# Attention: each unit's row maximum is rescaled on ScalarE instead of on VectorE

## The chip, the cores and the metric

One Trainium2 chip, and one of its cores does the whole computation. A core has five engines that run their own instruction streams and meet only at semaphores: TensorE (PE, matmuls and transposes; its weight loads are shown as PEld), VectorE (DVE), ScalarE (ACT), GpSimd (POOL) and SyncE (SP, which issues most of the DMAs). The metric is the device time of one execution in microseconds (us); the figure for a kernel is the median of its runs.

## The reference

The input `x` is 16 x 256 rows of 128 numbers. Three blocks are added to it in turn: a feed-forward block of eight experts (each row goes to the one expert with the highest gate logit), an attention block over 512 context keys with 8 heads, and the same feed-forward block again. All three read the layer norm of the current rows. The attention, which is what the change touches, is

```python
sim = einsum('hid,hjd->hij', qh, kh) * SCALE
mean = mean(sim, axis=-1)
sim = (sim - mean) * 1.5 + mean
attn = softmax(sim, axis=-1)
out = einsum('hij,hjd->hid', attn, vh)
```

for 4096 queries, 8 heads and 512 keys: 4096 x 8 x 512 scores, of which each row of 512 goes through a softmax.

## The kernel before

The span has three stages. In the first 143 us the attention weights are prepared and the first feed-forward block runs, 39 tiles of 128 rows one after another, sorted by expert. From 143 to about 634 us the attention runs. The rest is the second feed-forward block, whose routing (which row goes to which expert, at which place) is worked out while the attention runs.

The attention is cut into 256 *units*. Unit u belongs to group g = u // 32 (a group is 4 tiles of 128 queries, 512 queries together), to head h = (u // 4) % 8 and to tile or key chunk i = u % 4. For softmax the unit is one tile of 128 queries against all 512 keys of one head. For the product with the values the unit is one chunk of 128 keys against all 512 queries of the group, so it can start only when the four softmax units of its head are done.

Precision is that of fp32, made from fp16 pairs: a high part and a low part are kept of each operand and three matmuls are added (`three`, lines 1561 to 1563). So that the fp16 parts use their whole range, the operands are multiplied by powers of two that are computed from bounds on the data; `MUN` is the reciprocal power of two for the scores, one number for each partition in SBUF, that undoes this.

Each engine has a function `slot(n)` that is called for n = 0, 1, 2, ... and does a part of several units. What stands first in the function is issued first, and an engine never passes an instruction that waits:

- PE: scores of unit n (3 matmuls, lines 1561 to 1563, into one of three PSUM banks; waits until the exponential of unit n-3 is done). Then the value product of unit n-8 (3 matmuls, the same lines; at the first unit of a head it waits for `probsT_lo` of that head's last unit, n-5). Then the four transposes of unit n-3's probabilities (line 1785; they wait for the normalised probabilities of that unit, and for `probsT_lo` of unit n-5).
- DVE: `neg_max`, minus the row maximum of unit n's scores (line 1443), then `neg_max_unscaled`, that times `MUN` (line 1446), then `probsT_lo` of unit n-4 (line 1452, the transposed probabilities minus their fp16 high part; waits for ACT's high part), then `row_inv` of unit n-1 (line 1457).
- ACT: `probs` of unit n = exp(MUN * scores + neg_max_unscaled) with the row sum as a by-product (line 868), then `probsT_hi` of unit n-3 (line 877, the fp16 high part of the transposed probabilities).
- POOL: `probs` of unit n-1 times `row_inv` (line 642).

At fixed places of each group of 32 slots further work hangs on the end of a slot. On DVE: layer-norm statistics of the next group (slots 7 to 11 and 13), the residual rows of the last group (15 to 18), `xT_lo` (21, 22), statistics of the new rows (23 to 27), and the routing of the finished group (29 to 31 and 3 to 5 of the next). On ACT: `o_evac` (slot 8, line 896), four `ln_norm` (14 to 17, line 782), `ln_keep` (20, line 793), `x2T_evac` (22, line 902). On PE: four transposes each in slots 14, 19 and 20, the gate logits in 24 (line 1828) and the ranks in slot 1. On POOL: a power of 4 numbers a row in slots 12 and 28 (line 626 is the latter), for which DVE waits in slots 13 and 29.

The change touches the attention part of ACT's and DVE's `slot`. The semaphore `neg_max` is raised by line 1443 and `neg_max_ready` by line 1446; both `NM` and `NMS` have four columns, used in turn.

Of the kernel before, what the change touches and what calls it, by code (L numbers as in the profile page):

```python
# [8 lines left out]
def macaron_kernel(nc, x, context, Wq, Wk, Wv, Wout, bout, gate_w, gate_b, expert_bias, w1, b1, w2, b2, out):  # L9
# [13 lines left out]
    ALU = mybir.AluOpType  # L23
    ACT = mybir.ActivationFunctionType
# [39 lines left out]
    with ctx:  # L64
        def sb(name, shape, dt, where=ctx):
            return where.enter_context(nc.sbuf_tensor(name, shape, dt))

        def sem(name):
            return ctx.enter_context(nc.semaphore(name))
# [48 lines left out]
        NM = sb("neg_max", [P, 4], fp32)  # L118
        NMS = sb("neg_max_unscaled", [P, 4], fp32)
# [51 lines left out]
        with ExitStack() as att:  # L171
# [18 lines left out]
        MUN, VUN = (UNI[:, k:k + 1].bitcast(fp32) for k in range(2))  # L190
# [30 lines left out]
        neg_max_ready = sem("neg_max_unscaled_ready")  # L221
# [41 lines left out]
        scores, neg_max, probs, row_inv, normed = (sem("scores"), sem("neg_max_ready"), sem("probs_ready"),  # L263
                                                   sem("row_inv_ready"), sem("probs_normed"))
# [52 lines left out]
        def score_bank(u):  # L317

            return BK[u % 2] if u < FIRST_UNITS else BK[(6, 0, 1)[(u - FIRST_UNITS) % 3]]

        def turn_bank(job):

            return 4 + job % 2 if job else 1

        def unit(u):
            return 0 <= u < UNITS

        def after(n, s, back):

            g = n // HG - back  # L330
            return [g] if n % HG == s and 0 <= g < NG else []

        def ahead(n, s):

            return after(n, s, -1)
# [8 lines left out]
        def wait_rows(eng, r, j):  # L344

            if j >= CLOSE:
                eng.wait_ge(s_close, (SLOTS - CLOSE) * r + j - CLOSE + 1)
            else:
                eng.wait_ge(s_fin, CLOSE * r + j + 1)
# [337 lines left out]
        def _(act):  # L687
# [89 lines left out]
            def ln_norm(job, tiles_):  # L777
                act.wait_ge(ln_shift, job + 1)
                if job:
                    act.wait_ge(ln_T, job)  # L780
                for i in tiles_:
                    last = act.activation(XN[:, i, :], ROWS[:, G * job + i, 0:D], ACT.Identity, bias=SH[:, i:i + 1],
                                          scale=RS[:, i:i + 1])
                if i == G - 1:
                    last.then_inc(ln_xn, 1)
# [5 lines left out]
            def ln_keep(job, bank):  # L791
                act.wait_ge(ln_T, job + 1)
                act.activation(AXH[:, job % 2, :], BK[bank][:, :], ACT.Copy, scale=2.0 ** X_BITS)\
                    .then_inc(xT_hi, 1)
# [66 lines left out]
            def slot(n):  # L861
                if unit(n):
                    if n == 0:
                        act.wait_ge(s_hb, SLOTS)
                    act.wait_ge(neg_max_ready, n + 1)
                    if n >= 4:
                        act.wait_ge(pT_ps, n - 3)
                    act.activation(PR[:, n % 4, :], score_bank(n)[:, :], ACT.Exp, bias=NMS[:, n % 4:n % 4 + 1],  # L868
                                   scale=MUN, accum_out=SU[:, n % 4:n % 4 + 1]).then_inc(probs, 1)
                if unit(n - LAG_T):  # L870
                    u = n - LAG_T
                    act.wait_ge(pT_ps, u + 1)
                    if u == 0:
                        wait_rows(act, 0, SLOTS - 1)
                    if u % G == 0 and u // G >= 2:
                        act.wait_ge(av, G * (u // G) - G)
                    act.activation(PTH[:, (u // G) % 2, :, (u % G) * P:(u % G + 1) * P],  # L877
                                   BK[2 + u % 2][:, :].rearrange("p (c q) -> p c q", c=KC), ACT.Copy)\
                        .then_inc(pT_hi, 1)
                for i in range(G):  # L880
                    for g in ahead(n, 14 + i):
                        ln_norm(g, [i])
                for g in ahead(n, 20):
                    ln_keep(g, turn_bank(g))
                for g in after(n, 8, 1):
                    o_evac(g)
                for g in after(n, 22, 1):
                    x2T_evac(g)

            def o_evac(g):  # L890
                if g == 0:
                    act.wait_ge(bout_in, 16)
                act.wait_ge(av, HG * (g + 1))
                if g:
                    act.wait_ge(x2_logits, g)
                act.activation(XNT[:, :], BK[4 + g % 2][:, :], ACT.Identity, bias=BO[:, 0:1], scale=VUN)\
                    .then_inc(o_kept, 1)

            def x2T_evac(g):
                act.wait_ge(x2_T, g + 1)  # L900
                act.wait_ge(oT_ps, g + 1)
                act.activation(XNT[:, :], BK[router_bank(g, STAT_STEP)][:, :], ACT.Copy).then_inc(x2T_kept, 1)
# [7 lines left out]
        def _(dve):  # L910
            v = nc.vector
# [306 lines left out]
            def ln_stats(job, tiles_):  # L1218
                for i in tiles_:
                    last = v.bn_stats(BN[0][:, i, :], ROWS[:, G * job + i, 0:D])  # L1220
                if i == G - 1:
                    last.then_inc(ln_bn, 1)
# [12 lines left out]
            def ln_shift_of(job):  # L1235

                dve.wait_ge(ln_rstd, job + 1)
                v.scalar_tensor_tensor(out=SH[:, :], in0=MV[:, :, 0], scalar=-1.0, in1=RS[:, :],
                                       op0=ALU.mult, op1=ALU.mult).then_inc(ln_shift, 1)
# [200 lines left out]
            def slot(n):  # L1440
                if unit(n):
                    dve.wait_ge(scores, n + 1)
                    v.tensor_reduce(NM[:, n % 4:n % 4 + 1], score_bank(n)[:, :], AX.X, ALU.max, negate=True)\  # L1443
                        .then_inc(neg_max, 1)
                    dve.wait_ge(neg_max, n + 1)
                    v.tensor_scalar(NMS[:, n % 4:n % 4 + 1], NM[:, n % 4:n % 4 + 1], MUN, None, ALU.mult)\  # L1446
                        .then_inc(neg_max_ready, 1)
                if unit(n - LAG_T - 1):
                    u = n - LAG_T - 1
                    dve.wait_ge(pT_hi, u + 1)  # L1450
                    at = (slice(None), (u // G) % 2, slice(None), slice((u % G) * P, (u % G + 1) * P))
                    v.tensor_tensor(PTL[at], BK[2 + u % 2][:, :].rearrange("p (c q) -> p c q", c=KC),  # L1452
                                    PTH[at], ALU.subtract).then_inc(pT_lo, 1)
                if unit(n - 1):
                    u = n - 1
                    dve.wait_ge(probs, u + 1)
                    v.reciprocal(RI[:, u % 4:u % 4 + 1], SU[:, u % 4:u % 4 + 1]).then_inc(row_inv, 1)  # L1457

                for i in range(G):
                    for g in ahead(n, 7 + i):  # L1460
                        if n == 7:
                            dve.wait_ge(x1_in[1], 16 * (NG - 2))
                        if g == NG - 1 and i == 0:
                            dve.wait_ge(x1_in[2], 16)
                        ln_stats(g, [i])
                for g in ahead(n, 11):
                    ln_moments(g)
                for g in ahead(n, 13):
                    ln_shift_of(g)
                for half in range(2):  # L1470
                    for g in ahead(n, 21 + half):
                        xT_low(g, turn_bank(g), slice(half * 2 * P, (half + 1) * 2 * P))

                for i in range(G):
                    for g in after(n, 15 + i, 1):
                        new_row(g, i)
                    for g in after(n, 23 + i, 1):
                        x2_stats(g, i)
                for g in after(n, 27, 1):
                    x2_moments(g)  # L1480
                for g in after(n, 30, 1):
                    x2_shift_of(g)
                for i in range(3):
                    for g in after(n, 29 + i, 1):
                        onehot(g, range(3 * i, min(3 * i + 3, 8)))
                    for g in after(n, 3 + i, 2):
                        positions(g, [i])
                for i in range(14):
                    for g in after(n, 6 + i, 2):
                        if g == EARLY_GROUP:  # L1490
                            early_table(i)
# [395 lines left out]
```

## Time and profile before

| | us |
|---|---|
| median of 3 runs | 739.3 |
| the three runs | 738.98, 739.3, 742.73 |
| the profiled execution, its own time | 743.87 |
| its span in the trace | 742.0 |
| granted TensorE clock over the span, mean | 0.985 of full |

The trace is of one execution on the core. Its times count from the start of the span. Busy time of an engine is not its need: where a row says that an engine sat idle before an instruction, the number in brackets is that idle time and the name behind the arrow is what it waited for. An instruction may start before the end of the one ahead of it on the same engine, because they are pipelined; two starts tell the pace, and one duration tells the latency.

### The profile page before, as it was taken

The page shows a single profiled execution, that of the slowest core. Times are in us where ns is not written, and L with a number is a line of the kernel's source. Part 1 is how long each engine was busy: PE and PEld are TensorE (multiplying, and loading weights), DVE is VectorE, ACT ScalarE, POOL GpSimd, SP SyncE. Part 2 cuts the span into 40 slices and gives each one's busy share as a digit, 9 for nine tenths or more (in the row PEclk, how much of TensorE's full clock was granted, in tenths as well). Part 3 has the DMA queues.
Part 4 walks back from the last instruction along what each step waited for, and adds up shares of the span by engine and source line. Part 5 has one row for each costly group of instructions (what it writes and reads, how often), then busy time and mean ns, then how long its engine had stood idle before and what let it go on. Part 6 is the DMA issues. An engine that isn't in the chain of part 4 may idle for free.

```text
span 742.0 us, 15538 instructions
## 1 busy us (share of the span) xinstructions
PE 695.0 (94%) x4376; PEld 472.7 (64%) x4376; DVE 655.7 (88%) x1910; ACT 523.4 (71%) x1219; POOL 374.1 (50%) x507
## 2 busy tenths in 40 slices
PE   9988999989999999999999999999999998889992
PEld 7767888746556555655655655655565564669991
DVE  6989999998898999899899989899989987788882
ACT  4786777578778678778767867867876775546661
POOL 5066998344344345346346435534633633486662
PEclk9989999999999999999999999999999999999996
DMA  9951332210000000000000000000000011232210
GB/s 246 348 149 32 80 86 74 63 41 0 1 1 1 1 5 12 2 0 15 1 1 12 5 1 7 10 0 5 12 1 1 16 45 57 101 90 62 58 47 5
DMA packets 31794, 31.50 MB, mean 42 GB/s; under 512 B 5049, under 2 KB 26183, under 8 KB 31200
## 3 DMA queue, kind: packets, MB, share of 16 engines
q1 hardware_dynamic: 27360, 23.91, 11.0%
q0 software_dynamic: 3520, 6.40, 3.2%
q8 instruction: 38, 0.62, 0.4%
q14 instruction: 44, 0.36, 0.2%
q10 hardware_dynamic: 832, 0.21, 0.1%
HBM read 20.96 MB, written 10.47 MB: 42 GB/s over the span
## 4 chain that ended last, share of the span: by engine, by line
PE 47%; DVE 39%; issue 5%; POOL 2%; DMA 2%; ACT 1%; DVEq 1%; POOLq 0%; another core or an unknown queue 0%; SPq 0%; ACTq 0%
PE bank L1561 10%; DVE neg_max L1443 10%; PE bank L1563 9%; PE bank L1562 9%; DVE probsT_lo L1452 9%; PE bank L1785 9%; PE bank L1610 3%; DVE neg_max_unscaled L1446 3%; DVE hT_lo L1297 3%; PE bank L1596 2%; DVE slot_rows L1280 2%; DVE h L1276 2%; PE bank L1613 1%; DVE slot_rows L1289 1%; DMA rows<-in_L_attn_x 1%
## 5 line engine op out<-in xcount | busy, mean ns | idle before, releaser
L642 POOL TENSOR_SCALAR probs<-probs,row_inv 128x512 f32<-128x512 f32 x256 | 178.2, 697 | 266.1 <-DVE row_inv L1457 254.9
L868 ACT ACTIVATE probs<-bank,neg_max_unscaled,unscale_bits 128x512 f32<-128x512 f32 x256 | 199.2, 778 | 115.3 <-DVE neg_max_unscaled L1446 112.8
L1443 DVE TENSOR_REDUCE neg_max<-bank 128x1 f32<-128x512 f32 x256 | 175.9, 687 | 23.9 <-PE bank L1563 18.4
L1452 DVE TENSOR_TENSOR probsT_lo<-bank,probsT_hi 128x512 f16<-128x512 f32 x256 | 174.4, 681 | 3.3 <-ACT probsT_hi L877 3.2
L1785 PEld LDWEIGHTS bank<-ident,probs 128*128 128x128 f32 x1024 | 126.0, 141 | 65.9 <-issue 18.1
L1785 PE MATMUL bank<-ident,probs 128*128 128x128 f32 x1024 | 155.1, 274 | 8.6 <-DVE probsT_lo L1452 7.0
L877 ACT ACTIVATE probsT_hi<-bank 128x512 f16<-128x512 f32 x256 | 150.3, 587 | 3.2 <-PE bank L1785 3.2
L1561 PE MATMUL bank<-probsT_hi,vw_hi 128*128 128x512 f16 x256 | 98.1, 383 | 7.6 <-DVE probsT_lo L1452 6.7
L1562 PE MATMUL bank<-probsT_lo,vw_hi 128*128 128x512 f16 x256 | 97.5, 381 | 0.0
L1563 PE MATMUL bank<-probsT_hi,vw_lo 128*128 128x512 f16 x256 | 97.4, 380 | 0.0
L1561 PE MATMUL bank<-m_hi,xT_hi 128*128 128x512 f16 x256 | 97.0, 379 | 0.0
L1563 PE MATMUL bank<-m_hi,xT_lo 128*128 128x512 f16 x256 | 97.0, 379 | 0.0
L1562 PE MATMUL bank<-m_lo,xT_hi 128*128 128x512 f16 x256 | 97.0, 379 | 0.0
L1610 PE MATMUL bank<-w_hi_lo,hT_hi 128*128 x312 | 83.9, 346 | 10.5 <-DVE hT_lo L1297 6.3
L1613 PE MATMUL bank<-w_hi_lo,hT_lo 128*128 x312 | 69.7, 224 | 0.0
L1610 PEld LDWEIGHTS bank<-w_hi_lo,hT_hi 128*128 128x128 f32 x312 | 59.3, 190 | 16.1 <-issue 16.0
L818 ACT ACTIVATE hT_hi<-bank 128x512 fp32r<-128x512 f32 x78 | 46.6, 598 | 26.5 <-PE bank L1596 17.3
L1446 DVE TENSOR_SCALAR neg_max_unscaled<-neg_max,unscale_bits 128x1 f32<-128x1 f32 x256 | 54.8, 214 | 9.0
L1276 DVE TENSOR_TENSOR h<-bank,b 128x512 f32<-128x512 f32 x78 | 53.6, 687 | 9.6 <-PE bank L1563 7.4
L1613 PEld LDWEIGHTS bank<-w_hi_lo,hT_lo 128*128 128x128 f32 x312 | 60.3, 193 | 0.0
L1561 PEld LDWEIGHTS bank<-probsT_hi,vw_hi 128*128 128x128 f16 x256 | 25.0, 98 | 54.0 <-DVE probsT_lo L1452 30.9
L1297 DVE SCALAR_TENSOR_TENSOR hT_lo<-bank,hT_hi 128x512 fp32r<-128x512 f32 x78 | 53.0, 680 | 4.1 <-issue 2.1
(239 smaller groups left out, 1189.9 us busy)
## 6 DMA issues: line engine op xcount, KB each, us to landing
b<-in_L_ffn_b SPq DMA_DIRECT2D x4, 1024.0 KB, 9.1
x_packed<-slot_rows SPq DMA_DIRECT2D x39, 65.5 KB
slot_rows<-slots SPq DMA_DIRECT2D x39, 65.5 KB
x_stats<-rows SPq DMA_DIRECT2D x4, 524.0 KB, 10.5
rows<-x_packed SPq DMA_DIRECT2D x8, 262.0 KB, 2.6
rows<-in_L_attn_x SPq DMA_DIRECT2D x4, 512.0 KB, 8.6
w_lo<-in_L_ffn_w SPq DMA_DIRECT2D x8, 256.0 KB, 6.6
w_hi_lo<-in_L_ffn_w SPq DMA_DIRECT2D x8, 256.0 KB, 8.6
```

The costliest lines, as they stand in the source:

```text
L642: pool.tensor_scalar(PR[:, u % 4, :], PR[:, u % 4, :], RI[:, u % 4:u % 4 + 1], 2.0 ** P_BITS, ALU.mult, ALU.mult).then_inc(normed, 1)
L868: act.activation(PR[:, n % 4, :], score_bank(n)[:, :], ACT.Exp, bias=NMS[:, n % 4:n % 4 + 1], scale=MUN, accum_out=SU[:, n % 4:n % 4 + 1]) ...
L877: act.activation(PTH[:, (u // G) % 2, :, (u % G) * P:(u % G + 1) * P], BK[2 + u % 2][:, :].rearrange("p (c q) -> p c q", c=KC), ACT.Copy)\
L1443: v.tensor_reduce(NM[:, n % 4:n % 4 + 1], score_bank(n)[:, :], AX.X, ALU.max, negate=True)\
L1446: v.tensor_scalar(NMS[:, n % 4:n % 4 + 1], NM[:, n % 4:n % 4 + 1], MUN, None, ALU.mult)\
L1452: v.tensor_tensor(PTL[at], BK[2 + u % 2][:, :].rearrange("p (c q) -> p c q", c=KC), PTH[at], ALU.subtract).then_inc(pT_lo, 1)
L1561: pe.matmul(out_, wh, mh, start=start, stop=False)
L1562: pe.matmul(out_, wh, ml, start=False, stop=False)
L1563: return pe.matmul(out_, wl, mh, start=False, stop=stop)
L1610: pe.matmul(BK[6 + j % 2][:, 0:2 * D].rearrange("p (a s d) -> p a s d", a=1, s=2), HTH[:, j % 2, c * P:(c + 1) * P], W2HL[:, ds(e, 1), c, ...
L1613: last = pe.matmul(BK[6 + j % 2][:, 0:D].unsqueeze(1), HTL[:, j % 2, c * P:(c + 1) * P], W2HL[:, ds(e, 1), c, 0, :], start=False, stop=(c ...
L1785: last = pe.transpose(BK[2 + u % 2][:, c * P:(c + 1) * P], PR[:, u % 4, c * P:(c + 1) * P], IDN[:, :])
```

## The change

The multiplication of the row maximum by `MUN` moves from DVE, where it stands right behind the reduction, to ACT, where it stands right ahead of the exponential. It is an ACTIVATE with function Copy and the per-partition `MUN` as its scale, over 128 partitions x 1 element. ACT waits for the semaphore `neg_max` of the unit first, and then for its own multiplication through `neg_max_ready`, which it now raises itself. DVE loses the multiplication and the wait for its own reduction. Nothing else changes, and no data go another way.

```diff
@@ ACT, slot(n) @@
                 if unit(n):
                     if n == 0:
                         act.wait_ge(s_hb, SLOTS)
+                    act.wait_ge(neg_max, n + 1)
+                    act.activation(NMS[:, n % 4:n % 4 + 1], NM[:, n % 4:n % 4 + 1], ACT.Copy, scale=MUN)\
+                        .then_inc(neg_max_ready, 1)
                     act.wait_ge(neg_max_ready, n + 1)
                     if n >= 4:
                         act.wait_ge(pT_ps, n - 3)
@@ DVE, slot(n) @@
                     dve.wait_ge(scores, n + 1)
                     v.tensor_reduce(NM[:, n % 4:n % 4 + 1], score_bank(n)[:, :], AX.X, ALU.max, negate=True)\
                         .then_inc(neg_max, 1)
-                    dve.wait_ge(neg_max, n + 1)
-                    v.tensor_scalar(NMS[:, n % 4:n % 4 + 1], NM[:, n % 4:n % 4 + 1], MUN, None, ALU.mult)\
-                        .then_inc(neg_max_ready, 1)
                 if unit(n - LAG_T - 1):
                     u = n - LAG_T - 1
```

## Rows read from the trace of the kernel before

**Rows 1.** Windows, 160 to 620 us: us; busy PE, PEld, DVE, ACT, POOL; PEclk; DMA.
```profile
160.00:620.00 460.00, 448.70 (x2625) 267.33 (x2623) 421.77 (x1238) 351.69 (x782) 209.35 (x282) 1.00 0.02 6
```

**Rows 2.** Waits over the whole span: us in total, times, longest us.
```profile
ACT probs L868 <- DVE neg_max_unscaled L1446: 112.8, 197, 1.5
PEld bank L1561 <- DVE probsT_lo L1452: 30.9, 56, 1.6
```

**Rows 3.** PE by line and shape, 160 to 620 us: busy us, mean ns.
```profile
L1563 PE MATMUL bank<-m_hi,xT_lo 128*128 128x512 f16 x245 | 92.8, 379 | 0.0
L1828 PE MATMUL bank<-gate_wT,xn_then_xnT_or_oT 128*128 128x8 f32 x56 | 6.7, 246 | 0.0
```

**Rows 4.** Timeline of PE, one unit without extra work: start us, us, instruction.
```profile
277.19 0.60 PE L1785 MATMUL bank<-ident,probs 128*128 128x128 f32 x4
277.63 0.38 PE L1561 MATMUL bank<-m_hi,xT_hi 128*128 128x512 f16 x1
...
278.93 0.60 PE L1785 MATMUL bank<-ident,probs 128*128 128x128 f32 x4
```

**Rows 5.** Timeline of DVE, one unit without extra work.
```profile
271.48 0.69 DVE L1443 TENSOR_REDUCE neg_max<-bank 128x1 f32<-128x512 f32 x1
272.21 0.21 DVE L1446 TENSOR_SCALAR neg_max_unscaled<-neg_max,unscale_bits 128x1 f32<-128x1 f32 x1
272.34 0.68 DVE L1452 TENSOR_TENSOR probsT_lo<-bank,probsT_hi 128x512 f16<-128x512 f32 x1
272.93 0.15 DVE L1457 RECIPROCAL row_inv<-row_sum 128x1 f32<-128x1 f32 x1
```

**Rows 6.** Timeline of PE: waits for probsT_lo (in brackets), moments, then routing.
```profile
284.55 0.63 PE L1785 MATMUL bank<-ident,probs 128*128 128x128 f32 x4 [0.19 <-DVE probsT_lo L1452]
...
319.33 0.63 PE L1785 MATMUL bank<-ident,probs 128*128 128x128 f32 x4 [0.72 <-DVE probsT_lo L1452]
...
321.37 0.39 PE L1561 MATMUL bank<-probsT_hi,vw_hi 128*128 128x512 f16 x1 [0.76 <-DVE probsT_lo L1452]
```

**Rows 7.** Timeline of DVE: moments slot (280 to 283), then routing slots (310 to 322).
```profile
280.21 0.69 DVE L1443 TENSOR_REDUCE neg_max<-bank 128x1 f32<-128x512 f32 x1
...
282.88 0.68 DVE L1443 TENSOR_REDUCE neg_max<-bank 128x1 f32<-128x512 f32 x1
...
310.85 0.69 DVE L1443 TENSOR_REDUCE neg_max<-bank 128x1 f32<-128x512 f32 x1
...
316.89 0.19 DVE L1401 TENSOR_TENSOR logits<-bank,rows 128x32 f32<-128x32 f32 x1 [0.49 <-POOL rows L626]
...
321.67 0.68 DVE L1443 TENSOR_REDUCE neg_max<-bank 128x1 f32<-128x512 f32 x1
```

**Rows 8.** Timeline of ACT: a plain unit, then an o_evac.
```profile
272.45 0.78 ACT L868 ACTIVATE probs<-bank,neg_max_unscaled,unscale_bits 128x512 f32<-128x512 f32 x1 [0.37 <-DVE neg_max_unscaled L1446]
273.13 0.19 ACT L868 ACTIVATION_READ_ACCUMULATOR probs<-bank,neg_max_unscaled,unscale_bits 128x1 f32 x1
273.23 0.59 ACT L877 ACTIVATE probsT_hi<-bank 128x512 f16<-128x512 f32 x1
...
277.17 0.78 ACT L896 ACTIVATE xn_then_xnT_or_oT<-bank,bout,unscale_bits 128x512 f32<-128x512 f32 x1
```

**Rows 9.** ACT by line and shape, whole span: busy us, mean ns.
```profile
L721 ACT ACTIVATE m_hi<-m_raw,scale_bits 128x512 f16<-128x512 f32 x8 | 5.7, 709 | 0.0
L740 ACT ACTIVATE w_hi_lo<-w_hi_lo 128x512 fp32r<-128x512 f32 x8 | 4.9, 620 | 0.0
L782 ACT ACTIVATE xn_then_xnT_or_oT<-rows,shift,rstd 128x128 f32<-128x128 f32 x30 | 14.6, 491 | 0.0
L743 ACT ACT_TABLE_LOAD x1 | 1.3, 1283 | 2.7 <-issue 2.7
L743 ACT ACTIVATE row_sum<-ident 128x4 f32<-128x4 f32 x1 | 0.2, 206 | 0.0
```

**Rows 10.** Windows, where the last unit's transposes lie: columns as in Rows 1.
```profile
624.00:628.00 4.00, 3.02 (x10) 1.66 (x11) 2.11 (x9) 1.95 (x4) 1.39 (x2) 0.59 0.40 164
```

## The prediction

> **What bounds the kernel now.** I read the windows first. From 160 to 620 us, well inside the attention, PE is busy 448.7 of 460 us, DVE 421.8 and ACT 351.7, at full granted clock [rows 1]. So PE comes first, DVE is close behind, and ACT has room. Next the pace of PE where nothing disturbs it: from the transposes of one unit to those of the next is 278.93 - 277.19 = 1.74 us, and the four transposes take 277.63 - 277.19 = 0.44 of it [rows 4]. The grouped rows count 245 units in these 460 us, 1.88 us each [rows 3]. PE's extra work in 32 units is three times four transposes (0.44 each, as above) and the gate logits (6.7 / 7 = 0.96 at most [rows 3]), 2.3 us or 0.07 a unit. PE therefore needs 1.81 us a unit and takes 1.88: it loses 0.07 x 245 = 17 us here, and this is nearly all that a change on DVE or ACT can win.
>
> Then the waits, to see on whom PE loses it. PE's loads wait 30.9 us in all for `probsT_lo` of DVE [rows 2]; a load that waits ahead of a busy array costs nothing, so the total is no price, but the name is right. The PE timeline gives the price. Once in a group PE loses 0.19 + 0.16 = 0.35 us (0.16 being the 0.38 of a matmul that the 0.22 us pace hides, which a stop exposes) and, in the routing slots, 0.72 + 0.16 = 0.88 and 0.76 + 0.16 = 0.92 us [rows 6]. The last pair recurs in seven groups, the 0.35 in five. The rest is small: about 0.12 us ahead of each pair, 0.26 us in seven groups behind `xT_lo`, 0.06 us at most heads. ACT's big wait, 112.8 us for the rescaled maximum [rows 2], is no loss but room that ACT has, 0.37 us in a plain unit [rows 8].
>
> **What the change removes.** On DVE the reduction starts at 271.48 and `probsT_lo` at 272.34, 0.86 us later. `probsT_lo`, as wide, lets the next instruction start 0.59 us after its own start [rows 5]. Without the multiplication and the wait for the reduction, the 0.86 becomes about 0.61: **0.25 us a unit off DVE**, 64 us in 256 units of engine time. DVE's own pace falls from 0.86 + 0.59 + 0.07 = 1.52 to 1.27 us, plus the extra work of a slot. In a plain unit none of this is worth anything: DVE waits for PE anyway. It is worth something where extra work makes DVE late.
>
> **What it adds.** An ACTIVATE of one element a partition with a scale from SBUF. The trace has none, so I bound it. The lower end is 0.206 us, the 128x4 copy with constants; the upper end is 0.491 us, a 128x128 one with two operands from SBUF [rows 9]. I take 0.206 + (0.709 - 0.620) = **0.295 us**, the small copy plus what one scale from SBUF adds to a 128x512 copy, because width and operand are then both those of the new one; with the handover to the exponential, for which I take the 0.04 us between reduction and multiplication on DVE (271.48 + 0.69 to 272.21 [rows 5]), 0.33 us. The Trainium skill, "ScalarE: Activation LUTs", section "What ACT_TABLE_LOAD costs", says that an ACTIVATE with constants takes 186 ns and 0.833 ns an element, and each pointer operand 93 ns more; that is an estimate of 0.28 us, and the trace's 89 ns between the two copies agrees with it. The same page's "Rules for kernel authors" gives multiplications to VectorE; that rule speaks of the cost per element and here there is one element.
>
> Two things follow. First, latency: the exponential now starts 272.45 - 271.48 = 0.97 us after its reduction starts [rows 5, 8]; it will be 0.69 + 0.04 + 0.33 = 1.06, so 0.09 later. Second, ACT's pace: exponential to accumulator read 0.68, to `probsT_hi` 0.10, and about 0.49 (0.59 less the 0.10 overlap) until the next may start, 1.27 us [rows 8]. With 0.33 it is 1.60, against PE's 1.74. **ACT's margin falls from 0.47 to 0.14 us a unit.** Over a group ACT needs 32 x 1.60 + 4 x 0.39 (`ln_norm`, 0.491 less overlap [rows 9]) + 0.68 (`o_evac`, 0.78 less overlap [rows 8]) + about 1.0 (two 128x512 evacuations at 0.49) = 54.4 us; PE needs 32 x 1.74 + 2.3 = 58.0. ACT doesn't become the bound on the average; in slots with extra work it falls behind.
>
> Behind the waiting multiplication on ACT stand the exponential, `probsT_hi` and the evacuations, as they stood behind the waiting exponential. For `probsT_lo` of the next slot of DVE wait the value product and the transposes. In a plain unit `probsT_hi` ends 1.06 + 0.78 + 0.59 = 2.43 us after the reduction's start, so `probsT_lo` of the next slot can start at 2.47; today it starts at 1.74 + 0.86 = 2.60. So even with the longer ACT chain the thing that PE waits for comes 0.13 us earlier, and the 0.06 us losses go.
>
> **The sum.** Routing slots: five units take 321.67 - 310.85 = 10.8 us on DVE where PE needs 8.7 [rows 7]. I followed the five with the new gaps. Line 1401, which waits for POOL's power [rows 7], comes 0.41 us earlier, since that power itself stands behind a `row_inv` that is earlier by two gaps, less 0.09 where ACT's high part is awaited; the two slots behind add 0.23 and 0.24. `probsT_lo` is then 0.88 us earlier where PE stops for the second time: of 1.80 us lost, 0.9 stays. 7 x 0.88 = 6.2 us. Moments slot: 282.88 - 280.21 = 2.67 us [rows 7], two gaps of 0.21 to 0.25 lie ahead of the `probsT_lo` that PE stops for, more than the 0.35: 5 x 0.35 and a few of 0.11, 2.0 us. The 0.12 ahead of the pairs: 0.8. Of the rest (7 x 0.26, some 25 x 0.06 = 3.3) I take half, as ACT's evacuations lie there: 1.6. Gain 10.6 us.
>
> Against it, ACT's lateness. Behind `o_evac` ACT is 0.68 - 0.14 = 0.54 us late, two slots on 0.4, when the head at slot 12 needs its `probsT_lo`, which has a margin of some 0.1: 0.3 lost. Four `ln_norm` add 0.39 - 0.14 = 0.25 each, 1.0 in all, of which PE's own extra transposes in slots 14 and 19 give back 0.44 each: 0.1 lost at slot 20. So 0.4 us x 8 groups = 3.2 us. At the start of the stage PE has no value products, DVE sets the pace at 1.52 and ACT's 1.60 would replace it: 0.4 us. Net **7.0 us gained**: 743.9 becomes 736.9 for the profiled execution, and with the same 7.0 us off the median of the runs, which lies 4.6 us below that execution, 739.3 becomes 732.3; I say 732.
>
> One more term is left out of the sum. From 624 to 628 us the granted clock is 0.59 [rows 10], some 3.3 us at 1.2 GHz, where 1.6 us of work is lost; PE had stopped twice just before, for the last pair. If the shorter stops avoid it, 1.6 us more are gained. It goes into the range.
>
> **Rivals.**
> (a) *Everything hidden*: ACT's lateness costs nothing and PE keeps its 1.81 us pace throughout: 739.3 - 17 - 1.6 = 721. For it: ACT has 115 us of waits. Against it: the routing slots hold over 1 us of DVE work beyond PE's even without five multiplications. 0.07.
> (b) *ACT takes the place of DVE*, the slower side. It decides by the price of the new pair of instructions: at 0.47 us ACT's pace is PE's 1.74 and each evacuation's lateness is never caught up. With the upper end, 0.491 + 0.04, ACT needs 1.80 a unit and 32 x 1.80 + 3.2 = 60.8 us a group against today's 32 x 1.88 = 60.1, and `probsT_lo` comes later than now by 0.2 - 0.13, so the routing losses stay: with these 0.7 + about 0.6 us in 8 groups, 10 us lost, 749. For it: a dependent pair on ACT is not in the trace. Against it: the 0.206 row, only 0.09 below my price. 0.13.
> (c) *A wash*: at about 0.40 us the losses behind evacuations (some 1.2 us a group) eat the gain in the routing slots: 738 to 740. This also covers that the five slots follow ACT's chain and not DVE's. 0.20.
> (d) *A table load at each change between Copy and Exp*, 1.28 us each, would cost hundreds of us. Copy (line 877) and Exp alternate already and the one load is at the start [rows 9]: excluded. That the change doesn't do what it says can be left out too: it is two instructions moved.
>
> **How the numbers follow.** The forecast 0.60, its own range 728 to 736; (a) 0.07; (b) 0.13; (c) 0.20. Faster by over 0.5% (below 735.6): 0.57 of the forecast and all of (a) and a little of (c), 0.66. Within 0.5%, about what a measurement of this kernel can tell from no change: 0.21. Slower by over 0.5%: 0.13. The range 724 to 742 leaves out most of (a) and of (b).
>
> **What would show it.** The new ACTIVATE at 0.28 to 0.30 us; `probsT_lo` starting 0.61 us behind a reduction when late, and waiting for `probsT_hi` in plain units; exponentials 1.06 us behind their reductions; ACT's wait falling from 0.44 to some 0.1 us a unit; the pair of PE stops at 0.9 us together instead of 1.8, the moments stop gone, new stops of 0.1 to 0.3 at the heads behind `o_evac` and `ln_norm`. It is wrong if the ACTIVATE takes over 0.4, if ACT's chain stops PE at every head, or if DVE stays late for another reason.

## The result

The changed kernel takes **733.9 us** (median of 8 runs, 731.7 to 734.8), against 739.3 us for the kernel before (median of 8, 737.9 to 742.7). The ratio is 0.991, with an interval of 0.9894 to 0.9925: faster, by a little under 1%. Measured once more it was 732.4 against 739.7 us, ratio 0.9895 (0.9878 to 0.9913). 732 had been forecast.

The profiled execution of the changed kernel took 732.6 us, with a span of 730.8. Its windows from 160 to 620 us, with the columns of [rows 1]:

```profile
160.00:620.00 460.00, 450.02 (x2643) 270.47 (x2642) 395.06 (x1009) 418.92 (x1036) 210.59 (x285) 1.00 0.03 8
```

ACT and DVE have changed places: DVE was busy 421.8 us here and is now 395.1, ACT went from 351.7 to 418.9. PE gets through 2643 matmuls instead of 2625. The waits of the same stretch (us in total, times, longest):

```profile
ACT neg_max_unscaled L866 <- DVE neg_max L1446: 27.8, 52, 1.0
PEld bank L1561 <- DVE probsT_lo L1452: 27.7, 62, 1.4
...
DVE probsT_lo L1452 <- ACT probsT_hi L880: 26.4, 64, 0.6
```

ACT's wait for DVE is 27.8 us, where it had been 106.4 in the same stretch (112.8 over the span [rows 2]). The third row is new: 64 times DVE waits for ACT's high part, before only four times in the whole span. Where PE stopped for DVE in the routing slots [rows 6], it still stops, but for less (timeline of PE):

```profile
318.11 0.63 PE L1785 MATMUL bank<-ident,probs 128*128 128x128 f32 x4 [0.44 <-DVE probsT_lo L1452]
...
319.93 0.39 PE L1561 MATMUL bank<-probsT_hi,vw_hi 128*128 128x512 f16 x1 [0.54 <-DVE probsT_lo L1452]
...
378.26 0.63 PE L1785 MATMUL bank<-ident,probs 128*128 128x128 f32 x4 [0.44 <-DVE probsT_lo L1452]
```

0.72 and 0.76 have become 0.44 and 0.54. From one such first stop to that of the next group is 378.26 - 318.11 = 60.15 us; before it was 380.03 - 319.33 = 60.70.

To compare kernels I use the attention itself, from the start of the first score matmul to the start of the last one: 142.34 to 621.20, 478.9 us, before, and 142.89 to 616.29, **473.4 us**, after. Up to the last value product it is 491.6 and 484.3 us: 7.3 us less. These times can be compared across chips: two traces each of the changed kernel and of the one-pass kernel below give 473.4 and 473.6, 467.3 and 466.9 us. The spans differ by more, 11.2 us, of which 4.5 lie behind the last value product (108.1 and 103.6 us). I don't count that part as the change's: in the traces of the other kernels it varies between 103.4 and 110.1 us, it is 103.4 in one where DVE multiplies as before, and the profiled execution of before took 4.6 us more than its kernel's median. What makes it vary stays open.

### The profile page after: what moved, and what is told of

It is laid out like the page before. It is cut to its first block, busy times and chain, and to the rows that moved or that the text cites. A ratio compares the mean times of both kernels' runs of the same rounds, so it can differ in the third digit from the quotient of the medians.

```text
span 730.8 us, 15538 instructions
## 1 busy us (share of the span) xinstructions
PE 692.7 (95%) x4376; PEld 474.3 (65%) x4376; DVE 619.3 (85%) x1654; ACT 590.1 (81%) x1475; POOL 371.9 (51%) x507
## 4 chain that ended last, share of the span: by engine, by line
PE 52%; DVE 21%; issue 8%; ACT 7%; DMA 6%; POOL 4%; DVEq 1%; POOLq 0%; SPq 0%; ACTq 0%
PE bank L1561 12%; PE bank L1785 11%; PE bank L1563 11%; PE bank L1562 11%; DMA x_packed<-slot_rows 5%; DVE probsT_lo L1452 4%; DVE neg_max L1446 3%; DVE hT_lo L1300 3%; ACT probs L871 2%; ACT probsT_hi L880 1%; PE bank L1610 1%; DVE slot_rows L1283 1%; DVE slot_rows L1292 1%; DMA rows<-in_L_attn_x 1%; DVE slot_xT_lo L1305 1%
## 5 line engine op out<-in xcount | busy, mean ns | idle before, releaser
L1452 DVE TENSOR_TENSOR probsT_lo<-bank,probsT_hi 128x512 f16<-128x512 f32 x256 | 176.5, 689 | 33.2 <-ACT probsT_hi L880 29.2
L866 ACT ACTIVATE neg_max_unscaled<-neg_max,unscale_bits 128x1 f32<-128x1 f32 x256 | 75.1, 293 | 34.5 <-DVE neg_max L1446 29.3
L573 POOL DMA_INDIRECT slot_rows<-x_stats,row_of_slot x39 | 42.0, 1077 | 29.0 <-issue 26.1
```

Source lines behind the costliest of these rows:

```text
L866: act.activation(NMS[:, n % 4:n % 4 + 1], NM[:, n % 4:n % 4 + 1], ACT.Copy, scale=MUN)\
```

## The experiments

The theory at this point: PE's stops are set by two margins, DVE's in slots with extra vector work and ACT's behind its evacuations, and the change buys the first with the second. Rivals: that the length of the chain from reduction to high part is what counts; that the total of work moved counts and not its place; that ACT's part costs nothing. The times of the attention below are from first to last score matmul.

**Both halves apart.** The first kernel leaves the multiplication out on both engines:

```diff
                     act.wait_ge(neg_max, n + 1)
-                    act.activation(NMS[...], NM[...], ACT.Copy, scale=MUN).then_inc(neg_max_ready, 1)
-                    act.wait_ge(neg_max_ready, n + 1)
...
-                    act.activation(PR[...], score_bank(n)[:, :], ACT.Exp, bias=NMS[...], scale=MUN, ...)
+                    act.activation(PR[...], score_bank(n)[:, :], ACT.Exp, bias=NM[...], scale=ONF[:, 0:1], ...)
```

> The rescaling of the row maximum is left out on both engines: the exponential takes the unscaled maximum as bias and a scale of one from SBUF, so its probabilities are not those of the reference; everything else runs as in the changed kernel. Theory (DVE is relieved where it is late, ACT is made late behind its evacuations): ACT's pace is 1.27 us a unit again and DVE's stays at 1.27, so the stops of 0.27 at the head behind o_evac and 0.30 at the head behind the four ln_norm go, the moments stop shrinks from 0.25 to 0.1 or less, and the routing pair stays at 0.60 + 0.67, because line 1404 waits for POOL's power, which does not get faster. That is 0.8 to 1.0 us in each of 8 groups: 726 to 728 us. Rival (what counts is the whole chain from reduction to high part, 0.33 us shorter here): the routing pair falls too, below 0.6 in all, and the time is 721 to 723. Rival (ACT's lateness costs nothing): 733 to 734, as the changed kernel.

723.3 us against 739.0 for the kernel before, ratio 0.978 (0.9739 to 0.9814). The waits from 160 to 620 us:

```profile
ACT probs L868 <- DVE neg_max L1443: 98.1, 189, 1.5
DVE neg_max L1443 <- PE bank L1560: 58.0, 170, 1.0
PEld bank L1558 <- DVE probsT_lo L1449: 9.0, 12, 1.4
...
DVE probsT_lo L1449 <- ACT probsT_hi L877: 3.0, 11, 0.5
```

and the routing stops on PE:

```profile
314.18 0.63 PE L1782 MATMUL bank<-ident,probs 128*128 128x128 f32 x4 [0.18 <-DVE probsT_lo L1449]
316.00 0.39 PE L1558 MATMUL bank<-probsT_hi,vw_hi 128*128 128x512 f16 x1 [0.54 <-DVE probsT_lo L1449]
...
372.97 0.63 PE L1782 MATMUL bank<-ident,probs 128*128 128x128 f32 x4 [0.18 <-DVE probsT_lo L1449]
```

DVE waits for ACT's high part for only 3.0 us in all, where it was 26.4; the stops at the heads and in the moments slot are gone as expected, and the group takes 58.79 us, 0.8 us more than the 58.0 that I had worked out as PE's need. The second routing stop is the 0.54 of the changed kernel, as the theory said; the first fell from 0.44 to 0.18, which it had not said. There the chain rival is right in part, and the time lies 3 us under the lower end of the theory, just above that rival's 721 to 723. (0.15 us of the 0.26 are a longer DVE instruction beside a GpSimd one, shown further down with the moments stop.) ACT's multiplication costs more than I had thought: 723.3 to 733.9 us in medians, 464.1 to 473.4 in the attention.

The second kernel has the cost without the relief:

```diff
                     v.tensor_reduce(NM[...], score_bank(n)[:, :], AX.X, ALU.max, negate=True).then_inc(neg_max, 1)
+                    dve.wait_ge(neg_max, n + 1)
+                    v.tensor_scalar(NMS2[...], NM[...], MUN, None, ALU.mult)
```

> The changed kernel, and DVE also waits for its reduction and multiplies into a tile that nobody reads: the cost on ACT without the relief on DVE. Theory: DVE's 0.86 us from reduction to probsT_lo is back, the routing pair is 1.8 us again and the moments stop 0.35 or more, and ACT's stops (0.27, 0.30) stay: some 3 to 5 us above the kernel before, 742 to 745. Rival (the gain came from the shorter wait of the exponential, or from the clock, not from DVE's time): near the changed kernel, 734 to 736.

744.4 us, ratio 1.008 (1.0046 to 1.0114), as expected. Its routing stops are those of [rows 6] again:

```profile
322.15 0.63 PE L1788 MATMUL bank<-ident,probs 128*128 128x128 f32 x4 [0.71 <-DVE probsT_lo L1455]
324.19 0.39 PE L1564 MATMUL bank<-probsT_hi,vw_hi 128*128 128x512 f16 x1 [0.76 <-DVE probsT_lo L1455]
```

The four kernels together, attention time in us:

| | DVE multiplies | DVE doesn't |
|---|---|---|
| ACT doesn't | 478.9 (before) | 464.1 (neither) |
| ACT multiplies | 485.2 (both) | 473.4 (after) |

Relieving DVE is worth 14.8 us alone and 11.8 with ACT's part in place; ACT's part costs 6.3 or 9.3. The net of the change is 478.9 - 473.4 = 5.5 us, a small difference of two large terms. (In the upper right corner the exponential also comes earlier, so that corner holds a shorter chain as well as a relieved DVE.)

**How much room ACT has.** The multiplication twice on ACT, the first into a tile that nobody reads:

```diff
                     act.wait_ge(neg_max, n + 1)
+                    act.activation(NMS2[...], NM[...], ACT.Copy, scale=MUN)
                     act.activation(NMS[...], NM[...], ACT.Copy, scale=MUN).then_inc(neg_max_ready, 1)
```

> The changed kernel, with the multiplication on ACT issued twice in a row, the first into a tile that nobody reads. Theory: the first adds 0.20 us of pace and latency (0.293 less the 0.10 overlap), ACT needs 1.80 us a unit against PE's 1.74 and becomes the bound: 32 x 1.80 + 3.2 = 60.8 us a group plus what the moments and routing slots still cost, against 60.1 in the changed kernel: 8 to 14 us more, 742 to 748. Rival (ACT has room, since it waited 112.8 us before): under 2 us more.

749.1 us, ratio 1.0127 (1.0083 to 1.0171), attention 489.0: 15.2 us above the changed kernel's median, 1 us over the expected band. The timeline of ACT in it, two units:

```profile
272.38 0.29 ACT L868 ACTIVATE neg_max_unscaled<-neg_max,unscale_bits 128x1 f32<-128x1 f32 x1
272.70 0.78 ACT L873 ACTIVATE probs<-bank,neg_max_unscaled,unscale_bits 128x512 f32<-128x512 f32 x1
...
274.51 0.78 ACT L873 ACTIVATE probs<-bank,neg_max_unscaled,unscale_bits 128x512 f32<-128x512 f32 x1
```

274.51 - 272.70 = 1.81 us a unit, with no idle time on ACT: in these units it is the bound. 0.2 us more on ACT in each unit turn a gain of 5 us into a loss of 10. The changed kernel stands close to that edge.

**The third engine.** GpSimd multiplies from unit 4 on:

```diff
+                if unit(n) and not rescaled_by_act(n):
+                    pool.wait_ge(neg_max, n + 1)
...
+                    pool.tensor_scalar(NMS[...], NM[...], MUN, 1.0, ALU.mult, ALU.mult).then_inc(neg_max_ready, 1)
                 if n and unit(n - 1):
                     pool.wait_ge(row_inv, u + 1)
```

> GpSimd multiplies, from unit 4 on (ACT does it for units 0 to 3), ahead of its normalisation of the unit before; DVE and ACT are both relieved. Its price is not in any trace; by the reciprocal of 128x1 on DVE (0.15) and the 128x512 normalisation on POOL (0.69) I bound it by 0.1 and 0.7. Theory: with up to 0.37 us the exponential starts no later than in the changed kernel and the time is that of the run without any rescaling or up to 3 us above it, 726 to 731. If POOL takes over 0.6 us, the chain to probsT_hi is 0.3 us longer than in the changed kernel and PE stops at every head by about 0.2: 8 x 8 x 0.2 = 13 us more than 727, some 740.

759.3 us, ratio 1.026 (1.0223 to 1.0299): expectation missed by nearly 30 us, although the price was in my band. What I had not counted stands ahead of the multiplication in POOL's queue (timeline of POOL):

```profile
343.52 0.69 POOL L650 TENSOR_SCALAR probs<-probs,row_inv 128x512 f32<-128x512 f32 x1 [1.49 <-DVE row_inv L1468]
344.37 1.05 POOL L637 DMA_INDIRECT slots<-rows,pos  x1 [0.16 <-issue]
345.47 0.27 POOL L644 TENSOR_SCALAR neg_max_unscaled<-neg_max,unscale_bits 128x1 f32<-128x1 f32 x1
345.70 0.69 POOL L650 TENSOR_SCALAR probs<-probs,row_inv 128x512 f32<-128x512 f32 x1
```

The multiplication takes 0.27 us, but it stands behind a normalisation, which itself waits for DVE, and an indirect DMA of 1.05 us. It starts up to 2.7 us behind the end of its reduction, and ACT waits 136.2 us in all for it, 3.1 at the longest. A group takes 64.3 us. That POOL was busy half of the time said nothing about when it was free.

**Does the place decide?** Two complementary kernels. In the first ACT multiplies only where DVE is late, in the second only elsewhere:

```diff
+        def rescaled_by_act(n):
+            return n % HG in (11, 12, 13, 27, 28, 29, 30, 31, 0)
```

(the second has `not in`; whichever engine doesn't multiply leaves it to the other, with a count of its own).

> ACT multiplies only in the slots where DVE is late in the kernel before (11 to 13 and 27 to 31 of each group and 0 of the next), DVE in the other 23. Theory (place decides: DVE's relief is worth something only there, ACT's cost is paid behind its evacuations): the routing pair is that of the changed kernel, 0.60 + 0.70 us, the moments stop under 0.2, and the stops at the heads of slots 12 and 20 (0.27, 0.30) are not there; the 0.26 behind xT_lo in slots 21 and 22 is back. 0.3 to 0.5 us a group better than the changed kernel: 729 to 732. Rival (what counts is the total of DVE's relief): 9 of 32 units relieved give 9/32 of the effect, 737 to 738.

> The complement: DVE multiplies in slots 11 to 13, 27 to 31 and 0, ACT in the other 23. Theory: nothing of the relief in the routing slots, all of the cost behind the evacuations: the routing pair is 1.8 us, the moments stop 0.35, the stops at the heads of slots 12 and 20 0.3 each: 741 to 744, slower than the kernel before although 23 of 32 multiplications moved. Rival (the total counts): 23/32 of the effect of the change, 735 to 736.

The kernel before took 743.9 us on the chip of these four. The first: 734.8 us, ratio 0.988 (0.9844 to 0.9911), attention 471.8. The second: 744.6, ratio 1.0024 (1.0002 to 1.0047), attention 481.5. Both times lie above their bands, the first by 3 us, but so does the kernel before on this chip (743.9 against 739.3): by the ratios they are 730.3 and 741.1 us of 739.3, inside them. In the attention, nine multiplications of 32 moved to ACT gain 7.1 us over the kernel before, 1.6 more than all 32, and the other 23 lose 2.6 us. Shares of the change's 5.5 us by number would have been gains of 1.5 and 4.0. Place decides. The first routing stop of each:

```profile
317.31 0.63 PE L1795 MATMUL bank<-ident,probs 128*128 128x128 f32 x4 [0.37 <-DVE probsT_lo L1462]
```

```profile
321.45 0.63 PE L1795 MATMUL bank<-ident,probs 128*128 128x128 f32 x4 [0.72 <-DVE probsT_lo L1462]
```

Next, the changed kernel with only the seven slots behind an evacuation given back to DVE (`not in (9, 15, 16, 17, 18, 21, 23)`):

> The changed kernel, but DVE multiplies in the seven slots behind an evacuation on ACT (9, 15 to 18, 21 and 23 of each group). Theory: the stops at the heads of slots 12 and 20 (0.27 and 0.30 us) fall below 0.1 each, the moments stop (0.25) shrinks or goes, the routing pair stays at 1.3 us: 0.5 to 0.8 us a group, 728 to 730. Rival (the 9.8 us that ACT's multiplication costs are spread over all units by its longer chain): seven of 32 units give back 7/32 of them, 2 us: 732.

731.9 us, ratio 0.9846 (0.9813 to 0.988), attention 470.0: 3.4 us better than the changed kernel. That lies between the rival's 2 us and the theory's 4 to 6; a group in the middle of the attention takes 59.56 us, 0.57 less, inside the theory's band. The time in us, 731.9, is the rival's, but the kernel before is 4.6 us slower on this chip; by the ratio it is 727.9. On PE the stops at the heads of slots 12 and 20, which I read from the starts in its timeline, are 0.06 us at most; the moments stop is 0.22 instead of 0.25, and the routing stops are unchanged. So some 3.4 of the 9.3 us that ACT's part costs lie behind its evacuations. The rest lies mostly in the moments and routing slots, whose stops this kernel leaves nearly as they are.

**A version that pays on neither engine.** DVE can give the scaled, negated maximum in one instruction, the minimum over scores times minus `MUN` (`MNEG`, computed once at the start); ACT's multiplication goes too:

```diff
-                    v.tensor_reduce(NM[...], score_bank(n)[:, :], AX.X, ALU.max, negate=True).then_inc(neg_max, 1)
+                    dve.wait_ge(neg_max, n)
+                    v.tensor_scalar(SCD[:, :], score_bank(n)[:, :], MNEG, None, ALU.mult, ALU.min,
+                                    accum_out=NMS[...]).then_inc(neg_max, 1)
```

> DVE takes scaled and negated maximum in one instruction: scores times minus MUN into a tile that nobody reads, with the minimum as its accumulator. No engine multiplies afterwards. Its duration on DVE is in no trace; by the reduction (0.69) and probsT_lo (0.68, also from PSUM to fp16) and the accumulator read that ACT needs (0.19, of which 0.10 counts) I bound it by 0.69 and 0.88. Theory: at 0.70 to 0.79 the time is that of the run without rescaling or up to 3 us more, 723 to 727, because neither engine pays. If DVE pays 0.2 or more a unit for the accumulator, its 0.86 us from reduction to probsT_lo is back: 733 to 738.

729.3 us, ratio 0.981 (0.9785 to 0.984), attention 467.3: 3.2 us above the kernel without rescaling, at the upper end of the theory. The time in us lies above the band of 723 to 727, again on the slower chip. Its DVE timeline:

```profile
271.09 0.75 DVE L1448 TENSOR_SCALAR_CACHE_REDUCE scores_unscaled_unread<-bank,minus_unscale 128x512 f16<-128x512 f32 x1 [0.30 <-PE bank L1565]
271.77 0.08 DVE L1448 DVE_READ_ACCUMULATOR scores_unscaled_unread<-bank,minus_unscale 128x1 f32 x1
271.77 0.69 DVE L1454 TENSOR_TENSOR probsT_lo<-bank,probsT_hi 128x512 f16<-128x512 f32 x1
```

From its start to `probsT_lo` are 0.68 us: 0.18 less than before, 0.07 more than the 0.61 of a late slot in the changed kernel, and nothing on ACT. The change and this version on one chip:

> The changed kernel once more, on the same chip as the next, for a direct comparison: 0.991 of the kernel before, within its interval. From first to last score matmul of the attention, 473.4 us in its first profile, within 1 us of it.

> The kernel in which DVE takes the scaled and negated maximum in one instruction, once more. Theory: 6 us less than the changed kernel from first to last score matmul (467.3 against 473.4), so 0.8% below the changed kernel in time and 0.981 to 0.985 of the kernel before. If the gap is under 3 us, the earlier one was the chip's and not the kernel's.

The changed kernel: 732.4 us, ratio 0.9895 (0.9878 to 0.9913), attention 473.6. The one-pass kernel: **726.5 us**, ratio 0.981 (0.979 to 0.9826), attention 466.9, 5.9 us below the changed kernel (6.7 in the attention) and 13.2 below the kernel before. It beats both.

## Why the prediction was right, and where it was off

**The price** of the new instruction was taken as 0.295 us. By line and shape, 160 to 610 us of the changed kernel:

```profile
L866 ACT ACTIVATE neg_max_unscaled<-neg_max,unscale_bits 128x1 f32<-128x1 f32 x242 | 71.0, 293 | 31.1 <-DVE neg_max L1446 26.0
```

0.293 us: the small copy plus the difference between two wide ones was right to 2 ns. The estimate of 0.28 us from the Trainium skill, "ScalarE: Activation LUTs", section "What ACT_TABLE_LOAD costs", is 5% low. And the plain unit (timeline of ACT):

```profile
309.12 0.29 ACT L866 ACTIVATE neg_max_unscaled<-neg_max,unscale_bits 128x1 f32<-128x1 f32 x1
309.45 0.78 ACT L871 ACTIVATE probs<-bank,neg_max_unscaled,unscale_bits 128x512 f32<-128x512 f32 x1
```

The reduction started at 308.40, so the exponential comes 1.05 us behind it (1.06 forecast) and 0.33 behind the multiplication's start (0.33).

**DVE's gap** was to fall from 0.86 to 0.61 us where DVE is late. The routing slots of the changed kernel (timeline of DVE):

```profile
310.13 0.69 DVE L1446 TENSOR_REDUCE neg_max<-bank 128x1 f32<-128x512 f32 x1
...
312.42 0.68 DVE L1446 TENSOR_REDUCE neg_max<-bank 128x1 f32<-128x512 f32 x1
313.02 0.67 DVE L1452 TENSOR_TENSOR probsT_lo<-bank,probsT_hi 128x512 f16<-128x512 f32 x1
...
313.69 0.66 DVE L1446 TENSOR_REDUCE neg_max<-bank 128x1 f32<-128x512 f32 x1
314.85 0.69 DVE L1452 TENSOR_TENSOR probsT_lo<-bank,probsT_hi 128x512 f16<-128x512 f32 x1 [0.49 <-ACT probsT_hi L880]
...
315.77 0.19 DVE L1404 TENSOR_TENSOR logits<-bank,rows 128x32 f32<-128x32 f32 x1 [0.16 <-POOL rows L626]
316.00 0.55 DVE L1407 TENSOR_TENSOR logits<-logits,gate_b_expert_b 128x32 f32<-128x32 f32 x1
...
319.19 0.68 DVE L1452 TENSOR_TENSOR probsT_lo<-bank,probsT_hi 128x512 f16<-128x512 f32 x1
```

313.02 - 312.42 = 0.60. Line 1404 comes 315.77 - 310.13 = 5.64 us behind the first of the five reductions, where before it was 316.89 - 310.85 = 6.04 [rows 7]: 0.40 earlier, 0.41 forecast. The `probsT_lo` of the second stop comes 9.06 us behind, against 9.78 before (320.63 in the timeline): 0.72 earlier where 0.88 was forecast; 0.15 of the difference is line 1407 (line 1404 before), which takes 0.55 us here and 0.40 before. The pair of stops on PE fell from 1.80 to 0.44 + 0.54 + 2 x 0.16 = 1.3 us, where 0.9 was forecast.

**The moments stop** was to disappear. It fell only from 0.35 to 0.25 us, and this step failed. Before (timelines of DVE and, second row, POOL):

```profile
282.13 0.83 DVE L1233 TENSOR_SCALAR var_eps<-mean_var 128x4 f32<-128x4 f32 x1
282.24 0.70 POOL L642 TENSOR_SCALAR probs<-probs,row_inv 128x512 f32<-128x512 f32 x1
...
283.72 0.68 DVE L1452 TENSOR_TENSOR probsT_lo<-bank,probsT_hi 128x512 f16<-128x512 f32 x1
```

and in the changed kernel:

```profile
278.67 0.69 DVE L1452 TENSOR_TENSOR probsT_lo<-bank,probsT_hi 128x512 f16<-128x512 f32 x1 [0.53 <-ACT probsT_hi L880]
...
279.53 0.67 DVE L1446 TENSOR_REDUCE neg_max<-bank 128x1 f32<-128x512 f32 x1
280.24 0.69 DVE L1452 TENSOR_TENSOR probsT_lo<-bank,probsT_hi 128x512 f16<-128x512 f32 x1
...
281.31 0.99 DVE L1236 TENSOR_SCALAR var_eps<-mean_var 128x4 f32<-128x4 f32 x1
281.57 0.70 POOL L642 TENSOR_SCALAR probs<-probs,row_inv 128x512 f32<-128x512 f32 x1
...
282.81 0.68 DVE L1452 TENSOR_TENSOR probsT_lo<-bank,probsT_hi 128x512 f16<-128x512 f32 x1
```

I had given it two shorter gaps of DVE, 0.46 us. From the reduction to the `probsT_lo` that PE stops for it is 283.72 - 280.21 = 3.51 us before [rows 7] and 282.81 - 279.53 = 3.28 here: 0.23 less. Two things took the rest. I had forgotten that `probsT_lo` waits for ACT, which runs late there: 0.53 us ahead of this stretch, behind `o_evac`, and 0.10 in it (280.24 - 279.53 = 0.71 instead of 0.61). And line 1236 takes 0.99 us instead of 0.83. It ends 0.03 us behind POOL's normalisation (282.30 and 282.27; before 282.96 and 282.94), and so it does in every trace where that normalisation runs beside it, at lengths from 0.60 to 1.04 us. Line 1407 does the same in ten of the twelve traces, ending 0.03 to 0.05 us behind POOL's, at 0.55 us here and 0.40 before; in the two where it starts within 0.04 us of POOL's it takes 0.19. So these two small DVE instructions last until GpSimd's ends, and a DVE that comes earlier gains nothing on them; why is not shown. The kernel with neither multiplication has no such stop, with line 1233 at 0.83; the one that gives the slots behind `o_evac` back to DVE has line 1242 at 1.00, and its stop stays at 0.22.

**ACT's lateness** was forecast at 0.3 us at the head of slot 12 and 0.1 at that of slot 20. They are 0.26 and 0.31 (timeline of PE; the pace would have put the second row of each pair 0.22 behind the first):

```profile
280.50 0.38 PE L1563 MATMUL bank<-m_hi,xT_lo 128*128 128x512 f16 x1
280.98 0.39 PE L1561 MATMUL bank<-probsT_hi,vw_hi 128*128 128x512 f16 x1
...
296.02 0.38 PE L1563 MATMUL bank<-m_hi,xT_lo 128*128 128x512 f16 x1
296.55 0.39 PE L1561 MATMUL bank<-probsT_hi,vw_hi 128*128 128x512 f16 x1
```

**The terms of the sum** are where it was off. I had 10.6 us for the relief and 3.6 for ACT; in the attention up to the last score the runs give 14.8 and 9.3, or, taken in the other order, 11.8 and 6.3. The cost of ACT was summed over the two heads behind evacuations only: 0.4 us a group. By the groups of the changed kernel and of that without rescaling it is 60.15 - 58.79 = 1.36 us, and beside the two heads (0.57) there are the moments slot (0.25), the first routing stop (0.44 against 0.18, with 0.15 of it in line 1407) and some stops of 0.1. The relief was undersized because I took half of the small stops for lost; without rescaling they are gone. That both errors have one source, the 0.14 us of margin left on ACT, with which a late DVE must also catch up since each `probsT_lo` waits for a high part, is my reading and not shown by a run of its own. They nearly cancelled: the net is 5.5 us where 7.0 was forecast. That the time came out within 2 us of the forecast is in part this luck.

**The term left out** was paid. Up to the last value product the gain is 7.3 us, 1.8 more than up to the last score. The last pair of stops is 0.44 and 1.19 us instead of 0.71 and 1.41, and in the windows of after the granted clock stays at 1.00 from 616 to 626 us, where it had been 0.59 in 4 us [rows 10]:

```profile
616.00:626.00 10.00, 7.66 (x48) 4.12 (x46) 7.44 (x23) 6.28 (x15) 2.24 (x4) 1.00 0.46 159
```

The shorter stops give 0.3 of the 1.8 us and the clock 1.5: the kernel with both multiplications has last stops of 0.71 and 1.40 us, as before, at a granted clock of 1.00, and needs 11.2 us from the last score to the last value product, against 12.7 before and 10.9 after. Its windows, and those of the kernel in which ACT multiplies elsewhere, where the clock falls again behind stops of 0.72 and 1.41:

```profile
622.00:636.00 14.00, 11.46 (x70) 6.35 (x68) 11.54 (x37) 9.92 (x23) 5.21 (x7) 1.00 0.23 80
```

```profile
628.00:632.00 4.00, 3.83 (x18) 2.36 (x19) 1.98 (x7) 1.50 (x4) 1.39 (x2) 0.58 0.19 78
```

So of three traces with the long pair of stops two have the fall, and none of the nine others has it. That agrees with the forecast's reason, but one execution each can't prove it, and the third trace shows that the long stops don't always bring it.

**The rivals.** (b), ACT as the bound, is real, but 0.2 us of ACT away: the kernel with two multiplications is it, and at 749 us it lands on the price that (b) had. (c) had the slots following ACT's chain, which is true in part of the first routing stop and the moments slot; its 738 to 740 us isn't reached. (a) is refuted by the 9.3 us.

## What to carry to other kernels

When work moves from one busy engine to another, weigh both sides slot by slot: the relief counts only where the first engine is late, the cost wherever the second one is needed to catch up, and the net is a difference of two terms each larger than itself. An engine's idle total isn't free room: ACT waited 112.8 us here, and 75 us of new work on it (256 x 0.293) cost 6.3 to 9.3 us of time, most of it at single places where an evacuation or a late partner had used the margin already. Before moving a small operation, look whether the large one beside it can do it in passing: folding the scaling into the reduction gained about twice what moving it did (13.2 against 7.3 us on one chip).

## What the runs showed of the hardware

A 128x1 multiplication costs 0.21 us on DVE, 0.27 on GpSimd and 0.29 on ScalarE with a scale from SBUF. A DVE pass from PSUM with multiplication, a minimum as its accumulator and an fp16 output of 128x512 takes 0.75 us, against 0.69 for the plain reduction, and its accumulator read (0.08) starts together with the next instruction, so that the pair holds DVE for 0.68 us.

Two small DVE instructions from SBUF to SBUF (a 128x4 addition and a 128x32 one) that meet a GpSimd multiplication of 128x512 end 0.01 to 0.05 us behind it: they take 0.83 and 0.40 us in the kernel before, 0.99 and 0.55 in the changed one. The second takes 0.19 us where it starts together with GpSimd's.
